# A new order of the hops in a software-pipelined loop over 32 audio clips

## The reference, cut to what matters

```python
h = _L0_tok_ref(x, ...)                                   # conv, norm, relu x4; MLP; cumulative pooling
h = h + _L0_attn_ref(_layernorm(h, axis=-1), ...)         # r, k, v, decay, gate; state S over the rows; W_o
h = h + _L0_ffn_ref(_layernorm(h, axis=-1), ...)
# in _L0_ffn_ref:
kv_scores, indices = _pk(x, Wq_pk, pk_keys)               # per head: top 16 of 64 x 64 key pairs, softmax
ind = indices + offsets[None, None, :, None]
k = jnp.einsum('bnhk,bnhkd->bnhd', kv_scores, keys_table[ind])
v = jnp.einsum('bnhk,bnhkd->bnhd', kv_scores, values_table[ind])
attn = jax.nn.softmax(jnp.where(causal, sim, neg), axis=-1)
out = jnp.einsum('bhij,bjhd->bhid', attn, v)
return out.transpose(0, 2, 1, 3).reshape(b, n, HEADS * DIM) @ Wo
```

## Time and profile before

| | |
|---|---|
| median of 3 runs | 4099.62 us |
| the profiled execution | 4097.75 us |
| its span, first to last instruction | 4096.0 us |
| busy: PE, DVE, ACT, POOL | 3520.6, 2881.3, 2748.3, 2972.0 us |
| mean granted clock of PE | 0.927 of 2.4 GHz |
| HBM read and written | 214.36 and 1.05 MB, 53 GB/s |

### The profile page before, as it was taken

The page is one execution under the profiler, slowest core; times in us unless marked ns, Lnnn a source line. Parts: engine busy times, 40 slices in busy tenths (PEclk is TensorE's granted clock), DMA queues, the critical chain, the costliest instruction groups (busy, mean ns, idle before and its releaser), DMA issues.

```text
span 4096.0 us, 70697 instructions
## 1 busy us (share of the span) xinstructions
PE 3520.6 (86%) x20942; PEld 2637.9 (64%) x21258; DVE 2881.3 (70%) x13406; ACT 2748.3 (67%) x7874; POOL 2972.0 (73%) x3079
## 2 busy tenths in 40 slices
PE   8689999988889888889888889888889888888766
PEld 6366667666666666667666667666666666666655
DVE  2578777876777777677677777677777777677741
ACT  4477777776667677767677767667667667666533
POOL 0367777777777777777777777777777777777775
PEclk9799999999999999999999999998999998999877
DMA  3012222222222222222222222222222222222221
GB/s 113 25 49 53 53 54 53 53 53 54 53 54 54 53 52 54 53 54 54 53 52 54 53 53 53 54 53 52 54 53 54 54 53 52 54 53 53 53 53 42
DMA packets 108451, 220.15 MB, mean 54 GB/s; under 512 B 55769, under 2 KB 56193, under 8 KB 107553
## 3 DMA queue, kind: packets, MB, share of 16 engines
q0 software_dynamic: 98304, 201.52, 19.3%
q1 hardware_dynamic: 9760, 14.08, 1.0%
HBM read 214.36 MB, written 1.05 MB: 53 GB/s over the span
## 4 chain that ended last, share of the span: by engine, by line
POOL 41%; PE 18%; issue 15%; DVE 11%; ACT 9%; DMA 1%; DVEq 0%; POOLq 0%; ACTq 0%
POOL got L628 41%; PE bank L912 5%; PE bank L696 2%; ACT diag L1116 2%; PE bank L892 2%; PE bank L677 1%; DMA got<-in_table,rows 1%; DVE dist L1528 1%; ACT L942 1%; DVE pick L1524 1%; ACT d_exp L1095 1%; PE bank L682 1%; PE bank L870 1%; PE bank L906 1%; PE bank L871 1%
## 5 line engine op out<-in xcount | busy, mean ns | idle before, releaser
L628 POOL DMA_INDIRECT got<-in_table,rows x3072 | 2970.7, 967 | 1099.6 <-issue 922.8
L1116 ACT ACTIVATE diag<-cst,weight 128x128 f32<-128x128 f32 x3072 | 944.7, 393 | 21.8 <-PE bank L912 21.4
L912 PE MATMUL bank<-diag,got 128*128 128x128 f32 x6144 | 797.6, 292 | 51.0 <-DMA got<-in_table,rows 50.5
L912 PEld LDWEIGHTS bank<-diag,got 128*128 128x128 f32 x6144 | 766.7, 207 | 73.8 <-issue 61.0
L892 PE MATMUL bank<-d_w,tab 128*128 128x128 f32 x4096 | 647.3, 283 | 0.4 <-DVE d_w L1562 0.4
L1562 DVE SCALAR_TENSOR_TENSOR d_w<-bank,d_exp 128x256 f32<-128x256 f32 x1024 | 423.3, 421 | 287.5 <-ACT d_exp L1095 126.6
L892 PEld LDWEIGHTS bank<-d_w,tab 128*128 128x128 f32 x4096 | 554.1, 196 | 12.4 <-DVE d_w L1562 0.7
L1095 ACT ACTIVATE d_exp<-bank 128x256 f32<-128x256 f32 x1024 | 377.5, 376 | 169.3 <-PE bank L872 168.1
L870 PE MATMUL bank<-d_top,sel 128*128 128x512 bf16 x708 | 277.7, 392 | 92.3 <-DVE d_w L1562 90.2
L696 PE MATMUL bank<-h,conv_w 128*128 128x512 f32 (+2 forms) x1024 | 343.6, 484 | 11.9 <-DVE h L1226 8.1
L677 PE MATMUL bank<-wave,conv_w 25*128 25x512 f32 x256 | 177.9, 780 | 186.7 <-DVE normed L1201 170.4
(11 more groups left out here) (290 smaller groups left out, 6475.8 us busy)
## 6 DMA issues: line engine op xcount, KB each, us to landing
got<-in_table,rows POOLq DMA_INDIRECT x3072
tab<-in_table SPq DMA_DIRECT2D x2, 2048.0 KB, 16.1
got<-in_pairs SPq DMA_DIRECT2D x1, 2048.0 KB, 8.9
wave<-in_x SPq DMA_DIRECT2D x32, 50.0 KB
cst<-in_consts SPq DMA_DIRECT2D x1, 1059.0 KB, 7.3
mlp<-in_mw SPq DMA_DIRECT2D x1, 1024.0 KB, 9.5
out_h<-res_o SPq DMA_DIRECT2D x32, 32.0 KB
conv_w<-in_w SPq DMA_DIRECT2D x1, 512.0 KB, 3.9
```

The source lines that it names most:

```text
L628: pool.indirect_dma_start(got[:, g, k, :], None, table, bass.IndirectOffsetOnAxis(ap=rows[:, h * TOPK + k:h * TOPK + k + 1], axis=0)).then ...
L912: last = mm(kvt_ps, got[:, j % NGB, k, :], diag[:, j % NDG, k, :], start=k == 0, stop=k == TOPK - 1)
L1116: last = a(diag[:, (b * NG + h) % NDG, k, :], const("ident"), ACT.Copy, scale=weight[:, b % 2, h, k:k + 1])
```

## The change

The six lists of places in `AT` are replaced by other numbers. The hops, their groups, what each issues and every semaphore stay; each list still has one place for each hop, in rising order. So nothing is computed otherwise, and on every engine the same instructions come in another order.

```diff
@@ -450,34 +450,34 @@
 
         AT = (
             (
-                0, 12, 22, 27, 41, 48, 75, 101, 135, 161, 169, 183, 186, 195, 200, 253, 263, 265, 275, 287, 294,
...
+                0, 12, 24, 39, 108, 137, 140, 142, 159, 181, 195, 198, 214, 251, 260, 263, 280, 282, 294, 301, 313,
...
```

More of the change, by code:

```diff
@@ L452, in tower @@
             (
[3 rows of a table removed]
-            (
[5 rows of a table removed]
-            (
-                5, 34, 43, 60, 63, 89, 133, 137, 147, 193, 205, 222, 224, 227, 234, 236, 246, 292, 296, 304, 306,
-                308, 333, 342, 354, 381, 383, 398, 400, 402, 417, 429, 443),
-            (
[7 rows of a table removed]
-            (
-                10, 19, 36, 39, 51, 164, 214, 217, 299, 337, 357, 359, 361, 376, 407, 410, 728, 730, 764, 783, 786,
-                819, 882, 937),
-            (
[4 rows of a table removed]
[3 rows of a table added]
+            (
[5 rows of a table added]
+            (
+                5, 17, 29, 43, 55, 67, 82, 84, 128, 130, 145, 166, 173, 202, 205, 210, 212, 217, 219, 222, 284, 323,
+                325, 357, 373, 376, 378, 383, 386, 393, 402, 419, 422),
+            (
[7 rows of a table added]
+            (
+                10, 22, 34, 48, 60, 101, 188, 193, 253, 320, 330, 333, 535, 557, 571, 605, 655, 720, 788, 790, 793,
+                800, 889, 892),
+            (
[4 rows of a table added]
         )
```

## The result

The changed kernel takes 4123.8 us as a median (4115.6 to 4126.7, 6 runs) against 4098.0 of the kernel before on the same chip: a ratio of 1.0058, 95% interval 1.0045 to 1.007. It is slower, by 18 us more than I forecast and 5 us above the range. The profiled execution took 4124.0 us, with a span of 4121.4, 25.4 more than before.

The account below looks back on a forecast made before the run. POOL, full with its gathers, was taken to bound the kernel. 4097.75 + 7.0 (start) + 0 - 0.5 (tail) = 4104.3 us for the profiled execution, with 1.87 more 4106 as a median (+0.16%); range 4094 to 4119.

Parts of the forecast that it names:

- POOL is full; the engines' own loop costs nothing: Steady steps: POOL takes 122.10 us a batch without a stop, the engines' loop is 8.7 us shorter; cost 0.
- the rival's paragraph: Every step: engines' loop becomes the bound; 7 us lost gives 120.4, at 10 us 4136 to 4142; chance 0.08.
- Step 2 up to the second convolution: Step 2's quarters: moved scalings, nmax, squares and relu start the second convolution at 227.0 instead of 221.35, +5.6 us.
- From there to head 0's sum: Step 2, from the second convolution's start: +0.6 us for more half clock, +0.8 us up to head 0's sum.
- Behind the sum: POOL's wait at 287.42 for rows written 42.8 us behind head 0's sum: 0, from -1.0 to +2 us.
- I take 0, with +-7: POOL's pace over 30 batches: gathers meet DVE instructions at other places, same number; 0, with +-7 us.
- The rival "pace": POOL's pace alone moves by 0.35 us a batch, 10 us either way: 4116 (chance 0.08) or 4096 (0.06).
- The tail: After the last gather, 24.89 us: two last dense units' work moves ahead of head 5's sum; -0.5 us, at most 1.

Follow-up runs that it names:

- the run with an early sum: New table, but in step 2 head 0's sum stands right behind the second convolution; 4127.5 us, ratio 1.0072 to the kernel before.
- the one-input form: New table with L1524's additions of two SBUF tiles replaced by a scale and constant on one, changing the result; 4106.2 us, 1.0017 to the kernel before.

## Why the prediction was wrong

- **POOL is full; the engines' own loop costs nothing: right.** No gap above 0.31 us after 298, and the own loop at 119.4 is what the rival's paragraph gave for a 7 us displacement in every step (120.4), under POOL's pace.
- **Step 2 up to the second convolution: right.** Quarter 1's scaling 201.95 (202.9 predicted), nmax 207.19 (208.2), quarter 2's square 208.15 (209.3), quarter 3's product 213.95 (215.1), its relu 223.67 (224.9), the convolution 225.88 (227.0). Each is 0.9 to 1.2 us early, as the first gather is 1.1 us early. I had +5.6; measured from the first gather it is +5.65.
- **From there to head 0's sum: too small.** +0.6 and +0.8 predicted, +0.8 and +2.9 measured. 1.6 of the 2.1 us missing is the third convolution at a clock that had fallen again; I had given only the second a term for the clock. The rest is not taken apart.
- **Behind the sum: "I put it at 0", -1 to +2; it was +2.5.** And its reason was wrong: the wait at the 65th gather is not what sets batch 1, as the run with an early sum showed. It only happened that both moved alike. Why it was 2.5 stays open. Together the start cost 11.9 us, less the 1.1 by which all of it, from the first gather on, came earlier: 10.75 where I had 7.0.
- **"The new order meets gathers at other places, but with the same instructions in the same number [...] I take 0, with +-7": this step failed.** It measured +14.6 us; with this term at its 0 the range would have held. The instructions and the price of a hit on record (1.69 against 0.94) were right. The bound was not: I took the mean of 30 batches as if each were drawn anew, so that they would even out. But many hits come back in every step, and a shift of the mean does not even out: batches of one kernel differ in excess by 0.4 us (standard deviation), which would leave a mean of 30 independent ones uncertain by 0.1, and the two kernels' means lie 0.47 apart. What a batch can differ by (0.70 us for the slowest, or 2.02 to 2.77 of excess over the orders tried) is what the whole loop can differ by: over 31 batches a width of 23 us. The rival "pace" had this mechanism at 0.35 us a batch and a chance of 0.08; the truth was 0.47.
- **The Trainium skill's rule ("SBUF — State Buffer", Who interferes with whom)** says that whoever is first holds the shared ports. In the direction that DVE is first this trace agrees (L1313: 1.69 us). In the other direction it differs, and the measurement decides. I used the rule to say that DVE loses as often; it doesn't: a gather of 0.94 us that is first holds DVE up for 0.03 to 0.07 us, DVE the gather for up to 0.78 (1.72 instead of 0.94 at 2607.27 before), so nearly the whole cost is POOL's. The same section names single-input copies and tensor_scalar in a two-port mode as contending, and reductions as not. Both agree with what was measured, if the one-input form ran in such a mode, which no run shows: 65 gathers 0.19 us longer there, none longer under the reduction L1528 after the change.
- **The tail** moved by about +0.1 us, not -0.5.

## What to carry to other kernels

When the bounding engine never waits and yet its pace changes, look at the length of its instructions, and at what the neighbour on its ports was doing when each long one began. In a loop that one engine paces, a collision is not noise: it can repeat in every step, so bound it by the worst single step times the number of steps. And don't search orders for it but make the colliding instructions short: more and shorter instructions on an engine with room were worth 0.6% and 0.8 to 1.0% here, where the best of the orders tried brought 0.14%. And a wait is a cause only if removing it moves the end: put the work it waits for earlier once, and see whether the time goes or only changes its name.

## What I had not expected of the hardware

- A gather loses what is left of DVE's current instruction with two SBUF inputs less 0.127 us, and only of the current one, though the next follows without a pause.
- The two sides are unequal: 0.03 to 0.07 us for a DVE instruction whose start a gather beats, up to 0.78 the other way. An elementwise instruction with one SBUF input that ran at 0.44 us for 512 elements does it as well, and also costs a gather that began 0.15 to 0.20 us earlier 0.10 us.
- The granted clock fell to 0.57 in 240 to 244 of step 2 and eight products took 3.68 us instead of 2.09.
- The kernel before took 4096.7 to 4098.6 us in four groups of runs and 4108.7 in a fifth, on the chip that gave 4096.7 later. What it was stays open; it is as large as the effects here, so every ratio is taken within one group.
